# Moving the layer-norm deviation behind the last exponential of a step on ScalarE's queue

## What is computed

```python
q, k, v = proj(x, Wk, bk), proj(ctx, Wk, bk), proj(ctx, Wv, bv)      # 16 heads of 32
scores  = q @ k.T / sqrt(32)                                         # causal mask "allow"
p1      = softmax(where(allow, scores, NEG)) * allow                 # first exponential
dist    = sqrt(clip((p1.sum(-1) - cumsum(p1)) * abs(i - j), 0))
effect  = clip(exp(dist * -softplus(gammas)), 1e-5, 1e5)
attn    = softmax(where(allow, scores * effect, NEG))                # second exponential
x1      = layer_norm(x + (attn @ v) @ Wo.T + bo, ln1_w, ln1_b)       # deviation: 1/sqrt(var + eps)
out     = layer_norm(x1 + relu(x1 @ W1.T + b1) @ W2.T + b2, ln2_w, ln2_b)
```

## Time and profile before

| | |
|---|---|
| median of 3 runs | 1826.55 us (1825.06 to 1827.42) |
| profiled execution | 1825.06 us, span 1823.3 us |
| PE busy | 1540.7 us, 85% of the span |
| DVE busy | 1142.7 us, 63% |
| ACT busy | 936.4 us, 51% |
| POOL busy | 292.0 us, 16% |

### The profile page before, as it was taken

The page is one execution under the profiler, slowest core; times in us unless marked ns, Lnnn a source line. Parts: engine busy times, 40 slices in busy tenths (PEclk is TensorE's granted clock), DMA queues, the critical chain, the costliest instruction groups (busy, mean ns, idle before and its releaser), DMA issues.

```text
span 1823.3 us, 33263 instructions
## 1 busy us (share of the span) xinstructions
PE 1540.7 (85%) x11520; PEld 1220.0 (67%) x11520; DVE 1142.7 (63%) x3815; ACT 936.4 (51%) x2370; POOL 292.0 (16%) x252
## 2 busy tenths in 40 slices
PE   4778767867877887788787479999999999999996
PEld 4666546656655665566666358888888888888885
DVE  5999988989989888898988952322222222222223
ACT  1787776767768767676867732222222222222221
POOL 5001100100110010011000234130303030303030
PEclk9898888978978988898888789999999999999998
DMA  4001101101101110110100233010101010101000
GB/s 150 25 25 36 46 15 48 36 14 47 36 17 44 46 38 13 48 36 13 48 13 24 76 127 93 1 47 1 46 0 46 0 46 0 46 0 46 1 24 23
DMA packets 28871, 65.71 MB, mean 36 GB/s; under 512 B 2865, under 2 KB 2865, under 8 KB 28337
## 3 DMA queue, kind: packets, MB, share of 16 engines
q1 hardware_dynamic: 28720, 63.72, 10.2%
HBM read 46.94 MB, written 16.78 MB: 35 GB/s over the span
## 4 chain that ended last, share of the span: by engine, by line
PE 61%; DVE 29%; issue 7%; POOL 1%; ACT 0%; DVEq 0%; POOLq 0%; ACTq 0%
PE bank L228 18%; PE bank L229 17%; PE bank L230 17%; DVE sw_sb L852 6%; DVE sw_sb L863 5%; DVE sw_sb L837 4%; DVE sw_sb L825 3%; PE bank L481 3%; PE bank L463 3%; DVE sw_sb L858 2%; PE bank L493 1%; PE bank L503 1%; DVE cc_lo L887 1%; DVE cc_sb L883 1%; PE bank L375 1%
## 5 line engine op out<-in xcount | busy, mean ns | idle before, releaser
L1030 DVE TENSOR_TENSOR h_lo<-h_sb,h_hi 128x512 fp32r<-128x512 f32 x128 | 96.0, 750 | 519.5 <-ACT h_hi L741 519.5
L736 ACT ACTIVATE h_sb<-bank,b_col 128x512 f32<-128x512 f32 x128 | 88.3, 690 | 525.3 <-PE bank L230 525.3
L463 PE MATMUL bank<-qk_sb 32*32 32x256 f32 (+7 forms) x4096 | 177.4, 309 | 177.6 <-DVE m L825 161.9
L463 PEld LDWEIGHTS bank<-qk_sb 32*32 32x32 f32 x4096 | 117.7, 113 | 242.7 <-issue 212.5
L656 ACT ACTIVATE p_sb<-sw_sb,nm 128x32 f32<-128x32 f32 (+7 forms) x512 | 205.2, 407 | 43.6 <-DVE nm L868 43.1
L228 PE MATMUL bank<-ffw,h_hi 128*128 128x512 f32 x512 | 204.4, 399 | 2.9 <-DVE h_lo L1030 2.9
L228 PE MATMUL bank<-xt_hi,ffw 128*128 128x512 f32 x512 | 202.7, 396 | 1.0 <-DVE cc_sb L883 1.0
L230 PE MATMUL bank<-ffw,h_lo 128*128 128x512 f32 x512 | 203.3, 397 | 0.0
L229 PE MATMUL bank<-ffw,h_hi 128*128 128x512 f32 x512 | 203.2, 397 | 0.0
L229 PE MATMUL bank<-xt_lo,ffw 128*128 128x512 f32 x512 | 203.0, 396 | 0.0
L230 PE MATMUL bank<-xt_hi,ffw 128*128 128x512 f32 x512 | 202.7, 396 | 0.0
(11 more groups left out here) (124 smaller groups left out, 3280.3 us busy)
## 6 DMA issues: line engine op xcount, KB each, us to landing
x_raw<-x_t SPq DMA_DIRECT2D x16, 512.0 KB, 3.7
c_raw<-ctx_t SPq DMA_DIRECT2D x16, 512.0 KB, 4.5
xrow<-x_rows SPq DMA_DIRECT2D x16, 512.0 KB, 3.7
x_rows<-u_sb SPq DMA_DIRECT2D x16, 512.0 KB, 2.9
w_raw<-w SPq DMA_DIRECT2D x32, 256.0 KB, 3.0
x<-x_rows SPq DMA_DIRECT2D x8, 1024.0 KB, 8.0
out<-y_sb SPq DMA_DIRECT2D x7, 1024.0 KB, 5.3
sw_sb<-wk SPq DMA_DIRECT2D x1, 1024.0 KB, 4.9
```

The costliest lines, as they stand in the source:

```text
L463: mm = nc.tensor.matmul(s_bank[n % 2][rows, at:at + WIDTH[b]], qk_sb[rows, c % 2, 0, R * b:R * b + R], qk_sb[rows, c % 2, 1, S - WIDTH[b]: ...
L1030: nc.vector.tensor_tensor(h_lo[:, f % 2], h_sb[:, f % 2], h_hi[:, f % 2].bitcast(F32), ALU.subtract).then_inc(h_lo_ok, 1)
```

## The change

In ACT's step, two calls change places. `first_exp(i, c)` comes ahead of the `deviation(i - 2)` that quad 3 runs. All other engines' programs, all instructions and all semaphores stay as they are.

```diff
@@ -708,10 +708,10 @@
                         reciprocals(i - 1, c - 1)
                     if c == 3 and ahead:
                         qk_high(i + 1, 1)
+                    if now:
+                        first_exp(i, c)
                     if c == 3 and older:
                         deviation(i - 2)
-                    if now:
-                        first_exp(i, c)
                     if c == 0 and now:
                         qk_high(i, 2)
                     if last:
```

## The result

The changed kernel takes 1847.73 us (median, 1847.07 to 1851.22), the kernel before 1825.8 us beside it. The ratio of the two is 1.0124, with an interval of 1.0106 to 1.0141: slower by 21.9 us. The profiled execution after took 1849.49 us (span 1847.7), 24.4 us more than that of before.

What follows compares the result with a forecast made beforehand. The round of waits between PE, ACT and nearly full DVE was taken to bound the kernel. 13 steps x 2.44 us = 31.7 us, with 0 for the clock, added to 1826.55 us gave 1858 us, range 1850 to 1871.

Steps and rivals of the forecast that it cites:

- What bounds the kernel: Waits between PE, DVE and ACT set a step's length; DVE is nearly full, its longest wait `rstd`, 25.0 us in 13 times.
- Items 1 and 3: On ACT, the first exponential starts 0.43 us earlier and `turned` starts as before; each has value 0 on the path.
- Item 2: On ACT, `deviation` runs behind eight exponentials, so `rstd` and DVE's L915 come 2.44 us later.
- Item 4: On DVE, all work queued behind the waiting L915 comes 2.44 us later, and so do ACT and PE.
- Item 5: Between one deviation and the next, no slack takes the delay back: all 2.44 us stay, per step.
- Item 6: DVE's stall of about 3 us at the loop's turn, after steps 3, 5, 7, 9 and 11, moves along, swallowing nothing.
- Item 8: Step 15, with no batch ahead: the later deviation is covered by 1.1 us of DVE's work; value 0.
- The clock: PE's granted clock ahead of `rstd`: 1.37 us per slow step, taken as 0, bounds 5.5 us less to 12.3 us more.
- The rival of a worse clock: PE idles longer and its lower clock reaches the path: up to 1870.6 us; upper part of the full-price case, chance 0.91.

## Why the prediction was right in sign and too high

- *What bounds the kernel*: right. ACT's 0% of the chain hid a result that DVE waits for 13 times; moved ahead of ACT's wait, it gives 26.6 us, a part of them perhaps the clock's.
- *Items 1 and 3, no gain from the earlier exponential and `turned` unmoved*: right in the trace (3.48 against 3.45 us).
- *Item 2, 2.44 us for each deviation*: right; 2.44 and 2.45 us in the rows, and 2.45 us a step between steps at a like clock, with the added products.
- *Item 4, what is queued on DVE pays*: shown by the kernel that moves only those two instructions and is 42.9 us faster than the changed one. PE's wait at the begin of step 10, 4.70 us before, was forecast at 7.14 and is 7.19 us.
- *Item 5, nothing takes it back*: right for the waits, wrong as a whole. "Value: all 2.44 us stay, per step" holds for steps with a like clock alone.
- *Item 6, the loop's turn*: right; 15.6 us after, and the odd steps alone cost 17.6 us.
- *Item 8, step 15 is free*: right. From its L915 on, both profiles run the same: 24.53 us apart at step 14, 24.52 at step 15, 24.44 at step 17.
- *The clock*: this is the step that failed. "I see no reason for either direction and take 0", and its lower bound, 5.5 us, counted only the four slow ends, which the sizes of the wait for `rstd` show. Two more slow stretches lay in the middle of steps 7 and 12, where no wait of DVE for ACT is; they are seen in the lengths of the steps. All six went: 8.2 us. With six in the sum, its lower end would have been 1847.3 us and not 1850, and the term itself was 0 where it measured some -8. Of the waits, 25.0 + 31.7 = 56.7 us were forecast and 51.5 found; the 5.2 us between them are the four slow ends, to 0.3 us.
- *The rival of a worse clock*: the mechanism is real, the direction was the other for this change. The version with half of the delay shows it: all 12 middles low. Had the whole change gone the way of the half, the term of 0 would have been too small by 8.2 us in place of too large.

What stays open is why a step of 65.2 us plus one of 67.8 us keeps its slow stretches short when reached by 2.44 us of delay, and has one in every middle when reached by 1.23. That it depends on where PE's gaps fall is argued from the rows; no run here moved the gaps without changing their length. It is also striking that the full delay, half of it, and the whole in odd steps alone all bring two steps with a loop's turn to about 133.0 us, which a second limit of that length would do as well. Against such a limit: L915 waits for `rstd` in every one of these steps, and the one such pair of the odd-steps kernel with no slow stretch (steps 6 and 7) took 130.3 us.

## What to carry to other kernels

An engine with 0% of the chain may still make the result that closes it: look for a wait for it on the nearly full engine, and put the small instruction ahead of the long ones and ahead of waits for others. Before pricing an edit of a few us per round, compare the rounds of the kernel before with one another: when they differ by more than the price with the same instructions, split them by the granted clock of the stretches on the path, and bound the sum by all of them good and all of them bad. When doses of a delay don't cost in proportion, compare steps at the same granted clock, or add work that lifts it, and measure again.

## What the runs showed of the hardware

Four exponentials ahead of the deviation cost 24.3 us, all eight 21.9 us, which is the same within the noise: twice the delay cost nothing more, since the slow stretches of PE (granted clock 0.72 in place of 0.86) that came with the half were gone with the whole. And 31 products of 128x512 for each step, of no use to the result, made the kernel 36 us faster, as the granted clock at the steps' ends rose from 0.83 to 1.00.
